# One stage between the pass that sends by src and the first spreading: a graph network on Trainium2

## The chip, the cores and the metric

The kernel runs on one core of one Trainium2 chip. The metric is the device time of one execution in microseconds (us). The engines are TensorE (PE), VectorE (DVE), ScalarE (ACT), GpSimd (POOL) and SyncE (SP), which run at the same time and meet by semaphores. SP here only issues transfers; POOL issues the indirect ones.

## The reference

There are 12,500 nodes with 48 features and 400,000 edges. Four layers follow one another, each on a layer norm of the features. Cut to what matters here, the first is:

```python
h = jnp.maximum(_layernorm(x, axis=-1), 0.0)
xw = jnp.matmul(h, w)                              # L0: project, 48 x 48
msgs = edge_weight[:, None] * xw[src]
agg = jax.ops.segment_sum(msgs, dst, num_segments=12500)
x = x + jax.nn.relu(agg + b)
# L1 also needs, for each edge, emb[node_type[src]] and emb[node_type[dst]]
# L2: two rounds of x[src] * edge_weight summed by dst; L3: three such rounds (Chebyshev)
```

## The kernel before

Nodes are held by windows of 128: node n stands in partition n % 128 of window n // 128, so a tile of all features is `[128, 98, 48]`. Edges are sorted into blocks of 8 slots for each pair of windows; 554 groups of 128 blocks hold them, 4,432 slots in each partition.
The part that the change touches stands between two long passes:

- The pass that sends by src (`recc`, `sent`, L887 to L975). SP loads records of edges two groups at a time (`recc`), ACT and DVE pick fields, and POOL sends a row of each block to `sent_dram` with 554 indirect transfers (L969).
- Stage 1 (L998 to L1052). SP loads the sent rows (`sent_in`: 554 pieces of 17 numbers in each partition). The places of dst and of src (`drel`, `srel`) are turned from partition to row: 35 tiles of each, PE transposes one 128 by 128 tile in float32 (L1023), ACT copies it to bfloat16 (L1032), SP stores it (L1042), with two buffers, so that a copy waits for the store before last. POOL gathers the type embeddings of each window (`uv`, inside `tab0`) with 98 indirect transfers (L1049).
- Stage 2 (L1601): DVE fills `X` with zeros.
- Stage 3 (`node_block`, L1088). SP loads `x` into `X`, DVE makes the layer norm (`layernorm`, L1075 to L1085) with the square root on ACT (L1104), and copies types into `rest0` and `evs`; POOL stores `evs`.
- Stage 4 (`project`, L1132). 25 spans of four windows: PE transposes (L1142), ACT copies (L1172), PE multiplies by `w0` (L1153), DVE puts the product into `rest0` (L1622).
- Stage 5: DVE splits `rest0` into three bfloat16 terms, the table `tab0` (`split`, L1194 to L1198).

Then comes the first spreading (`expand`), which multiplies one-hot matrices of places by the table, weighs the rows and sends them off, and after it the passes of the four layers.

Of the kernel before, what the change touches and what calls it, by code (L numbers as in the profile page):

```python
# [10 lines left out]
P = 128  # L11
# [64 lines left out]
def gnn_kernel(nc, x, src, dst, edge_attr, edge_weight, node_type, node_vec, w0, b0, w1, b1, w2, b2,  # L76
# [64 lines left out]
    with ctx:  # L141
# [729 lines left out]

        CS = CH * B
# [3 lines left out]
        with ExitStack() as s2:  # L876
# [12 lines left out]
            with nc.Block() as block:  # L889
                @block.sync  # L890
                def _(sp):
                    sp.dma_start(delta[:, :], delta_dram.rearrange("(a d) s -> a (d s)", a=1).to_broadcast([P, W * W])
                                 ).then_inc(s_delta, 16)

# [33 lines left out]
                def _(dve):  # L928
# [49 lines left out]
        X = sb("X", [P, W, D])  # L978
# [6 lines left out]
        s_uvg = sem("types_gathered")  # L985
        with ExitStack() as s2:
            sent_in = scoped(s2, "sent_in", [P, NG, SENT], F32)
            beyond = scoped(s2, "beyond", [P, NG], F32)

            srel_f = h1[:, :, :].rearrange("p w f -> p (w f)")[:, 0:NS]  # L990
            drel_f = X[:, :, :].rearrange("p w f -> p (w f)")[:, 0:NS]
            assert NS <= W * D
            turned = scoped(s2, "places_turned", [P, 2, P], BF16)
            ps_p = s2.enter_context(nc.psum_tensor("ps_p", [P, 2, 512], F32))
            s_ld, s_cp, s_tr, s_ev = (sem(f"rows_{n}") for n in ("load", "copied", "trans", "turned"))
            s_st = sems("rows_store", 2)
            NTR = ceil_div(NS, P)
            with nc.Block() as block:  # L998
                @block.vector
                def _(dve):  # L1000
                    dve.tensor_copy(drel_f[:, :], drel[:, :, :, 0].rearrange("p g k -> p (g k)")).then_inc(s_cp, 1)
                    dve.wait_ge(s_ld, 16)
                    dve.tensor_copy(srel_f[:, :].rearrange("p (g k) -> p g k", k=B),
                                    sent_in[:, :, 0:B]).then_inc(s_cp, 1)
                    dve.tensor_scalar(less_ident_b[:, :], ident_b[:, :], -1.0, None, ALU.mult)
                    dve.tensor_copy(slots[:, 0:NS].rearrange("p (g k) -> p g k", k=B), sent_in[:, :, B:2 * B])

                    dve.tensor_scalar(beyond[:, :], sent_in[:, :, 2 * B], 0.0, BIG, ALU.is_equal,
                                      ALU.mult).then_inc(s_cp, 1)
                    dve.wait_ge(s_cp, 3)  # L1010
                    with nc.allow_low_precision(reason="block numbers: whole, below 2^24"):
                        dve.scalar_tensor_tensor(out=idx_d[:, :], in0=sent_in[:, :, 2 * B], scalar=-1.0,
                                                 in1=beyond[:, :], op0=ALU.add, op1=ALU.add)

                @block.tensor
                def _(pe):
                    for t in range(2 * NTR):
                        of, n = (drel_f, t) if t < NTR else (srel_f, t - NTR)
                        m = min(P, NS - n * P)
                        pe.wait_ge(s_cp, 1 + t // NTR)  # L1020
                        if t >= 2:
                            pe.wait_ge(s_ev, t - 1)
                        pe.transpose(ps_p[0:m, t % 2, 0:P], of[:, n * P:n * P + m], ident[:, :]).then_inc(s_tr, 1)  # L1023

                @block.scalar
                def _(act):
                    for t in range(2 * NTR):
                        m = min(P, NS - t % NTR * P)
                        act.wait_ge(s_tr, t + 1)
# [968 lines left out]
```

## Time and profile before

| | before |
|---|---|
| median of three runs | 16256.79 us (16254.69 to 16295.25) |
| the profiled execution's own time | 16257.53 us |
| its span, first to last instruction | 16255.7 us |
| DVE busy | 12042.7 us, 74% of the span |
| PE busy | 10843.7 us, 67% |
| POOL busy | 7855.1 us, 48% |
| ACT busy | 7461.2 us, 46% |

Busy shares are means over passes of different kinds and say little about one stage; the part between the two passes is some 300 us long and is read by itself. A row of the timeline has the start, the duration, the engine, the line and the operation, and in brackets how long the engine had been idle and what released it. A row of SPq is the time that SP took to issue a transfer, and not the transfer.

### The profile page before, as it was taken

The numbers are of one execution on the slowest core, as the hardware profiler recorded it, in microseconds if no ns is written. First come the engines' busy times: TensorE is split into PE (matmuls) and PEld (weight loads), VectorE is DVE, ScalarE is ACT, GpSimd is POOL, SyncE is SP. The second block draws the span as 40 slices with busy tenths as digits, with TensorE's granted clock in tenths as the row PEclk, the third lists the DMA queues.
The fourth block names the chain that finished last, engine by engine and source line by source line (L and its number), as shares of the span: only waits on it lengthen the run. The fifth ranks groups of instructions, "written<-read, shape, count | busy, mean of one in ns | idle before, by whom it ended". The sixth has DMA issues, their size and how long they took to land. (4 is left out here: it accounts for less than half of the span.)

```text
span 16255.7 us, 582040 instructions
## 1 busy us (share of the span) xinstructions
PE 10843.7 (67%) x194032; PEld 8861.6 (55%) x194033; DVE 12042.7 (74%) x25807; ACT 7461.2 (46%) x21291; POOL 7855.1 (48%) x7665
## 2 busy tenths in 40 slices
PE   5676666666610488867776677777776686676678
PEld 4555555555500366644555556666655565565556
DVE  9666666666633378789996788789778778777776
ACT  0121212121122267744445656766664475475466
POOL 0677777777777366013331067037307605713730
PEclk8777777777755599988888888999997797798789
DMA  8343333333467499879998798889779898988987
GB/s 339 111 124 124 123 123 123 123 123 123 123 170 179 114 364 350 291 257 341 331 309 246 241 337 324 280 307 353 274 261 375 319 313 332 373 277 309 384 289 238
DMA packets 1719990, 4103.19 MB, mean 252 GB/s; under 512 B 337506, under 2 KB 626240, under 8 KB 1719094
## 3 DMA queue, kind: packets, MB, share of 16 engines
q1 hardware_dynamic: 1288470, 3065.78, 57.2%
q0 software_dynamic: 431248, 1034.11, 16.5%
q8 instruction: 80, 1.31, 0.0%
q10 hardware_dynamic: 144, 1.60, 0.0%
q14 instruction: 48, 0.39, 0.0%
HBM read 2932.16 MB, written 1702.21 MB: 285 GB/s over the span
## 5 line engine op out<-in xcount | busy, mean ns | idle before, releaser
L1443 POOL DMA_INDIRECT messages<-exp_stage,exp_block_rows x3324 | 3555.9, 1070 | 4461.9 <-ACT exp_stage L1423 1830.6
L845 POOL DMA_INDIRECT records<-rec,row_i x3125 | 3113.0, 996 | 1444.6 <-issue 814.5
L1584 PEld LDWEIGHTS sum_sums<-sum_slots,sum_onehot 128*128 128x128 bf16 x93072 | 2521.5, 96 | 1135.8 <-issue 1133.7
L1584 PE MATMUL sum_sums<-sum_slots,sum_onehot 128*128 128x48 bf16 (+1 forms) x93072 | 2677.8, 183 | 625.6 <-DVE h L1510 485.3
L1541 ACT ACTIVATE sum_onehot<-iota_b,sum_late_places 128x128 bf16<-128x128 bf16 x5817 | 1910.1, 391 | 765.1 <-PE sum_sums L1584 681.0
L1301 PE MATMUL exp_rows<-tab,h 128*128 x39888 | 1811.7, 197 | 512.7 <-DVE h L1342 225.2
L1307 PE MATMUL exp_rows<-tab,h 128*128 x13296 | 1428.4, 282 | 932.1 <-ACT exp_stage L1423 688.0
L1301 PEld LDWEIGHTS exp_rows<-tab,h 128*128 128x128 bf16 x39888 | 1567.7, 102 | 872.5 <-issue 726.5
L1307 PEld LDWEIGHTS exp_rows<-tab,h 128*128 128x128 bf16 x13296 | 1208.5, 125 | 1151.8 <-issue 1118.9
L668 ACT COPY rec<-emeta 128x40 f32 (+1 forms) x625 | 140.2, 224 | 3064.3 <-DMA records<-rec,row_i 3064.3
L1342 DVE TENSOR_SCALAR h<-exp_places,pcol 128x2048 bf16<-128x2048 bf16 x1662 | 1298.9, 782 | 164.4 <-DMA exp_places<-src_places 140.7
L789 PE MATMUL ps_l<-place_high,turned 98*128 98x98 f16 x3125 | 506.4, 258 | 1229.4 <-DVE place_low L723 1227.7
L739 DVE TENSOR_REDUCE row_i<-rank 128x5 int32<-128x490 f32 x625 | 414.0, 662 | 1206.1 <-ACT rec L668 1205.1
L1843 POOL DMA_INDIRECT messages<-l_back,l_rows x554 | 544.8, 983 | 1563.5 <-ACT l_back L1718 836.4
L1510 DVE TENSOR_TENSOR h<-h,sum_sums 128x48 f32 x3324 | 678.0, 204 | 713.4 <-PE sum_sums L1584 460.1
L1351 DVE TENSOR_TENSOR exp_times<-exp_rows,slots 128x384 f32<-128x384 f32 x1662 | 934.5, 562 | 338.7 <-PE exp_rows L1301 189.2
L1379 DVE CAST exp_stage<-exp_rows 128x576 bf16<-128x576 f32 x1380 | 990.9, 751 | 254.7 <-DMA messages<-exp_stage,exp_block_rows 181.2
L1548 ACT ACTIVATE sum_onehot<-sum_onehot,one_col 128x384 bf16<-128x384 bf16 x1939 | 1161.6, 599 | 0.0
L686 DVE TENSOR_SCALAR same<-win_row,emeta 128x640 bf16<-128x640 bf16 (+4 forms) x3125 | 1091.6, 349 | 3.3 <-DMA win_row<-src_windows_of_edges 3.3
L1402 ACT CAST exp_stage<-exp_times 128x384 bf16<-128x384 f32 x1662 | 799.2, 481 | 642.2 <-DVE exp_times L1351 623.8
L789 PEld LDWEIGHTS ps_l<-place_high,turned 98*128 98x128 f16 x3125 | 377.4, 127 | 1292.5 <-DVE place_low L723 1291.8
L1423 ACT CAST exp_stage<-exp_rows 128x576 bf16<-128x576 f32 x1662 | 992.0, 638 | 127.5 <-PE exp_rows L1307 124.0
(299 smaller groups left out, 22128.4 us busy)
## 6 DMA issues: line engine op xcount, KB each, us to landing
sum_slots<-messages SPq DMA_DIRECT2D x1662, 576.0 KB, 5.3
exp_places<-src_places SPq DMA_DIRECT2D x1662, 512.0 KB
sum_slots<-messages SPq DMA_DIRECT2D x277, 600.0 KB, 5.4
messages<-zeros SPq DMA_DIRECT2D x124, 1149.0 KB
l_places<-dst_places SPq DMA_DIRECT2D x277, 512.0 KB, 6.3
recc<-records SPq DMA_DIRECT2D x277, 448.0 KB, 4.7
l_gate<-records SPq DMA_DIRECT2D x277, 448.0 KB
records<-fill SPq DMA_DIRECT2D x215, 576.0 KB, 12.9
```

The lines of the kernel that those rows point to most:

```text
L686: return dve.tensor_scalar(same[:, g, j, j * P:K * P], win_row[:, g, j * P:K * P], emeta[:, bass.ds(n * K, K), :][:, j, SWIN:SWIN + 1], No ...
L845: pool.indirect_dma_start(rec_dram, bass.IndirectOffsetOnAxis(ap=row_i[:, g, k:k + 1], axis=0), rec[:, g, k, :], None).then_inc(put[g], 16)
L1301: last = pe.matmul(rows_at(u, a, k), of, flat[:, bass.ds(ws[c * CH + g] * (3 * width) + j * width, width)], start=j == 0, stop=j == 2)
L1307: last = pe.matmul(got[:, u % NW, k // 2, at:at + 3 * D], of, flat[:, bass.ds(ws[c * CH + g] * (3 * D), 3 * D)], start=True, stop=True)
L1342: dve.tensor_scalar(onehot[:, c % RS, :, :].rearrange("p n e -> p (n e)"), places[:, c % RP, :], pcol1[:, :], None, ALU.is_equal).then_inc ...
L1351: dve.tensor_tensor(left(u), rows_of(u, 0, D), ews[:, bass.ds(i * (2 * RG) + 2 * (c * CH + n), 2), :].unsqueeze(3) .to_broadcast([P, 2, BH ...
L1379: dve.tensor_copy(*copy_out(dve, i, first, c - 1, n)).then_inc(x_out[1], 1)
L1423: act.copy(*copy_out(act, i, first, c, n)).then_inc(x_out[0], 1)
L1443: pool.indirect_dma_start(lines, bass.IndirectOffsetOnAxis(ap=row_d[:, c, g:g + 1], axis=0), stage[:, c, g, :], None, element_offset=0 if ...
L1541: last = act.activation(late(c)[:, n, :], iota1_b[:, :], ACT.Abs, bias=late_rel[:, c, n:n + 1], scale=-1.0)
L1548: act.activation(late(c), late(c), ACT.Relu, bias=one_col[:, :], scale=-1.0).then_inc(g_late, 1)
L1584: last = pe.matmul(sums[:, c % RS, g, 0:width], onehot[:, c % RS, g * B + k, :], of[:, n * width:(n + 1) * width], start=n == 0, stop=n == ...
```

## The change

The five stages become one block of code, and the load of `x` moves into the pass ahead.

- The zeroing of `X` and the two loads of `x` go to the start of the pass that sends by src: SP issues them behind `delta` and ahead of the first `recc`.
- The places are turned in bfloat16, four tiles to one bank, one copy and one store: 10 batches instead of 35 for dst and as many for src. dst is read where it lies; src is copied to bfloat16 first.
- `project` gets `ahead` and `behind`: work of each engine before and after its own. Ahead of it stand the layer norm, the turning of dst, the load of `sent_in` and the gather of types; behind it stand the turning of src, the copies of types and the split.
- The gather is waited for by DVE behind the projection.

The core of the diff (`layernorm`, `split` and `expand` are as they were):

```diff
@@ the pass that sends by src
                     sp.dma_start(delta[:, :], ...).then_inc(s_delta, 16)
+                    sp.wait_ge(s_x0, 1)
+                    sp.dma_start(X[:, 0:W - 1, :], x[0:full].rearrange("(w p) f -> p w f", p=P)).then_inc(s_x, 16)
+                    sp.dma_start(X[0:TAIL, W - 1, :], x[full:N]).then_inc(s_x, 16)
...
+                    dve.memset(X[:, :, :], 0.0).then_inc(s_x0, 1)
                     dve.wait_ge(s_delta, 16)
@@ the stage
+                def turn_places(pe, b, of):
+                    at, many, m = batches[b % NTR]
+                    if b >= 2:
+                        pe.wait_ge(s_ev, b - 1)
+                    for j in range(many):
+                        last = pe.transpose(ps_p[0:m, b % 2, j * P:(j + 1) * P], of(at + j * P, m), ident_b[:, :])
+                    last.then_inc(s_tr, 1)
+
+                def copy_places(act, b):
+                    _, many, m = batches[b % NTR]
+                    act.wait_ge(s_tr, b + 1)
+                    if b >= 2:
+                        act.wait_ge(s_st[b % 2], 16 * (b // 2))
+                    act.copy(turned[0:m, b % 2, 0:many * P], ps_p[0:m, b % 2, 0:many * P]).then_inc(s_ev, 1)
+
+                def vector_ahead(dve):
+                    node.append(Node(dve))
+                    dve.wait_ge(s_x, 32)
+                    node[0].layernorm(h1[:, :, :], X[:, :, :], square, True)
+                    mark["x"] = node[0].c.n
+                    dve.wait_ge(s_ld, 16)
+                    dve.tensor_copy(srel_b.rearrange("p (g k) -> p g k", k=B), sent_in[:, :, 0:B]).then_inc(s_cp, 1)
...
+                def vector_behind(dve):
+                    c = node[0].c
+                    dve.wait_ge(s_uvg, 16 * W)
                     c(dve.tensor_copy(rest0[:, :, D:T0], uv[:, :, 0:G]))
                     c(dve.tensor_copy(evs[:, :, :], uv[:, :, G:2 * G]))
                     mark["evs"] = c.n
                     c.done()
+                    dve.wait_ge(s_tr, 2 * NTR)
+                    split(c, dve, tab0, rest0[:, :, :], rest0[:, :, :])
...
+                def tensor_ahead(pe):
+                    for b in range(NTR):
+                        turn_places(pe, b, lambda at, m: drel_b[:, at:at + m, 0])
+                    pe.wait_ge(v, mark["x"])
+
+                def tensor_behind(pe):
+                    pe.wait_ge(s_cp, 1)
+                    for b in range(NTR, 2 * NTR):
+                        turn_places(pe, b, lambda at, m: srel_b[:, at:at + m])
+
+                def scalar_ahead(act):
+                    for b in range(NTR):
+                        copy_places(act, b)
+                    for at, a, _ in node[0].acts:
+                        act.wait_ge(v, at)
+                        act.activation(a, a, ACT.Sqrt).then_inc(s_node, 1)
...
+                def sync_ahead(sp):
+                    sp.dma_start(sent_in,
+                                 sent_dram.rearrange("(g p) f -> p g f", p=P)).then_inc(s_ld, 16)
+                    for b in range(2 * NTR):
+                        to = drel_dram if b < NTR else srel_dram
+                        at, many, m = batches[b % NTR]
+                        sp.wait_ge(s_ev, b + 1)
+                        sp.dma_start(to[at:at + many * m, :].rearrange("(j p) e -> p j e", p=m),
+                                     turned[0:m, b % 2, 0:many * P].rearrange("p (j e) -> p j e", e=P)
+                                     ).then_inc(s_st[b % 2], 16)
```

On ACT, between the pass that sends by src and the first spreading, this stood before (`places_turned` is the buffer of turned places, `var` the variances under the root, `lhs` the turned features of a span):

```order
L1032 CAST places_turned<-ps_p 128x128 x34
L1032 CAST places_turned<-ps_p 80x128
L1032 CAST places_turned<-ps_p 128x128 x34
L1032 CAST places_turned<-ps_p 80x128
L998 UNCONDITIONAL_BRANCH
L1100 UNCONDITIONAL_BRANCH
L1104 ACT_TABLE_LOAD
L1104 ACTIVATE var<-var 128x98
L1088 UNCONDITIONAL_BRANCH
L1164 UNCONDITIONAL_BRANCH
L1172 COPY lhs<-pst 48x512 x24
L1172 COPY lhs<-pst 48x256
```

And this stands there now:

```order
L1586 COPY places_turned<-ps_p 128x512 x8
L1586 COPY places_turned<-ps_p 128x256
L1586 COPY places_turned<-ps_p 80x128
L1633 ACT_TABLE_LOAD
L1633 ACTIVATE var<-var 128x98
L1132 COPY lhs<-pst 48x512 x24
L1132 COPY lhs<-pst 48x256
L1586 COPY places_turned<-ps_p 128x512 x8
L1586 COPY places_turned<-ps_p 128x256
L1586 COPY places_turned<-ps_p 80x128
```

The root still stands behind the copies of dst, now in one block of code with them; the copies of src moved behind those of the projection.

On SP, at the start of the pass that sends by src (`delta` is a table of shifts, `recc` the records, `X` the features), this stood before and stands now:

```order
L892 DMA delta<-shift_of_blocks 128x9604
L901 DMA recc<-records 128x2x448 x6
```

```order
L895 DMA delta<-shift_of_blocks 128x9604
L898 DMA X<-in_x 128x97x48
L899 DMA X<-in_x 84x48
L907 DMA recc<-records 128x2x448 x6
```

The two loads of `X` came between the table and the first records.

## Rows read from the trace of the kernel before

**Rows 1.** Windows: stretch and length, busy us of each engine, granted clock, DMA share, GB/s.

```profile
4568.00:5298.40 730.40, 0.00 (x0) 0.00 (x0) 233.96 (x1662) 185.29 (x1385) 541.44 (x556) 0.50 0.74 186
5298.40:5596.20 297.80, 99.97 (x364) 67.92 (x364) 83.89 (x48) 34.40 (x97) 99.00 (x99) 0.50 0.37 48
5596.20:16255.70 10659.50, 7685.44 (x164872) 6232.83 (x164872) 8487.08 (x15640) 6415.00 (x17281) 4100.63 (x3878) 0.87 0.88 311
```

**Rows 2.** Timeline around the start of stage 1: start, duration, engine, line, operation.

```profile
5298.58 0.85 SPq L1036 DMA_DIRECT2D sent_in<-laces_weights_and_blocks  x1
...
5301.88 52.29 SPq L1042 DMA_DIRECT2D dst_places<-places_turned  x1
...
5355.88 2.77 POOL L1049 DMA_INDIRECT tab<-table_types,types_i  x1 [0.30 <-issue]
5356.07 2.47 DVE L1003 COPY h<-sent_in 128x4432 f32<-128x4432 f32 x1 [55.05 <-DMA sent_in<-laces_weights_and_blocks]
5357.19 0.64 ACT L1032 CAST places_turned<-ps_p 128x128 bf16<-128x128 f32 x2 [55.12 <-DMA dst_places<-places_turned]
```

**Rows 3.** The tile `places_turned`: its copies on ACT, durations in ns, first and last start.

```profile
L1032 ACT CAST places_turned<-ps_p x70: 262/266/267, 5301.6 to 5422.8; 128x128 bf16<-128x128 f32 x68, 80x128 bf16<-80x128 f32 x2
```

**Rows 4.** The end of stage 1 (L998) on POOL's queue: duration in ns, start.

```profile
L998 POOLq DRAIN  x1: 8045/8045/8045, 5429.1 to 5429.1; - x1
```

**Rows 5.** Timeline of stages 2 and 3, zeroing, load and layer norm.

```profile
5438.40 3.98 DVE L1604 MEMSET X<- 128x4704 f32 x1 [75.66 <-issue]
5442.66 1.28 ACT L1104 ACT_TABLE_LOAD   x1 [19.63 <-PEq L1601]
5442.72 11.66 SPq L1109 DMA_DIRECT2D X<-in_x  x2
5456.28 5.05 DVE L1075 TENSOR_REDUCE mean<-X 128x98 f32<-128x4704 f32 x1 [13.90 <-DMA X<-in_x]
...
5477.13 0.29 ACT L1104 ACTIVATE var<-var 128x98 f32<-128x98 f32 x1 [33.19 <-DVE var L1080]
...
5483.42 2.61 DVE L1085 TENSOR_SCALAR h<-h 128x4704 f32<-128x4704 f32 x1
...
5487.77 1.79 DVE L1614 COPY evs<-tab 128x3136 f32<-128x3136 f32 x1
```

**Rows 6.** Timeline of stage 4, the projection, its first and last work.

```profile
5495.93 1.87 PE L1142 MATMUL pst<-ident,h 128*48 128x128 f32 x8 [74.30 <-PEq L1088]
5496.98 0.58 ACT L1172 COPY lhs<-pst 48x512 f32<-48x512 f32 x1 [19.57 <-PE pst L1142]
...
5565.61 0.26 DVE L1622 COPY rest<-pso 128x96 f32<-128x96 f32 x1 [0.50 <-PE pso L1153]
```

**Rows 7.** Timeline of stage 5, the split, and the first load behind it.

```profile
5566.19 4.25 DVE L1194 CAST tab<-rest 128x7840 bf16<-128x7840 f32 x1 [0.32 <-PEq L1132]
...
5591.46 4.24 DVE L1198 CAST tab<-rest 128x7840 bf16<-128x7840 f32 x1
5596.19 13.69 SPq L1254 DMA_DIRECT2D exp_places<-src_places  x7
```

**Rows 8.** Windows: DVE's five operations on the sent rows, and the projection.

```profile
5356.00:5366.00 10.00, 4.10 (x10) 1.82 (x10) 6.64 (x5) 2.66 (x10) 8.78 (x5) 0.50 0.22 46
5496.00:5566.00 70.00, 69.57 (x294) 55.22 (x294) 8.84 (x25) 14.26 (x25) 0.00 (x0) 0.50 0.00 1
```

**Rows 9.** Timeline of the pass that sends by src, its first and last work.

```profile
4583.58 0.22 ACT L913 COPY sent<-recc 128x16 f32<-128x16 f32 x1 [53.89 <-DMA recc<-records]
...
4585.34 1.01 POOL L969 DMA_INDIRECT laces_weights_and_blocks<-sent,row_s  x1 [16.06 <-ACT drel L917]
...
5293.14 0.97 POOL L969 DMA_INDIRECT laces_weights_and_blocks<-sent,row_s  x1 [0.30 <-issue]
```

**Rows 10.** That pass's indirect transfers on POOL, durations in ns, first and last start.

```profile
L969 POOL DMA_INDIRECT laces_weights_and_blocks<-sent,row_s x554: 971/972/1070, 4585.3 to 5293.1; - x185
```

**Rows 11.** Transfers issued at 4566 to 4584 us: number, size, us to landing.

```profile
delta<-shift_of_blocks SPq DMA_DIRECT2D x1, 4802.0 KB, 14.2
```

More of the change, by code:

```diff
@@ L870, in windows @@
                 skip_runtime_bounds_check_because="windows are counted below W")[1]
+        X = sb("X", [P, W, D])
+        s_x0, s_x = sem("x_zeroed"), sem("x_load")
+        full = (W - 1) * P
         CS = CH * B
@@ L1121, in gnn_kernel, with project @@
         n_pj = [0]
-        def project(parts, put, room=None):
+        def project(parts, put, room=None, ahead={}, behind={}):
             base = PT * n_pj[0]
@@ L1132, in project, with _ @@
                 with nc.Block() as block:
+                    @block.vector
+                    def _(dve):
+                        if "vector" in ahead:
+                            ahead["vector"](dve)
+                        for n, (w0, w1) in enumerate(spans):
+                            dve.wait_ge(pj_prod, base + n + 1)
+                            put(dve, pso[:, n % 2, 0:(w1 - w0) * D].rearrange("p (w f) -> p w f", f=D),
+                                slice(w0, w1)).then_inc(pj_out, 1)
+                        if "vector" in behind:
+                            dve.wait_ge(pj_out, base + PT)
+                            behind["vector"](dve)
+                    if "sync" in ahead:
+                        block.sync(ahead["sync"])
+                    if "gpsimd" in ahead:
+                        block.gpsimd(ahead["gpsimd"])
                     @block.tensor
@@ L1173, in _ @@
                             last.then_inc(pj_lhs, 1)
-                    @block.vector
-                    def _(dve):
-                        for n, (w0, w1) in enumerate(spans):
-                            dve.wait_ge(pj_prod, base + n + 1)
-                            put(dve, pso[:, n % 2, 0:(w1 - w0) * D].rearrange("p (w f) -> p w f", f=D),
-                                slice(w0, w1)).then_inc(pj_out, 1)
+                        if "scalar" in behind:
+                            behind["scalar"](act)
         x_ld, x_st = sems("exp_load", RC), sems("exp_store", RC)
@@ L1589, in _ @@
                         turns_and_rest(pe, TURNS, REST, turn)
-        full = (W - 1) * P
+        s_uvg, s_evs = sem("types_gathered"), sem("dst_embedding_stored")
+        s_ld, s_cp, s_tr, s_ev = (sem(f"rows_{n}") for n in ("load", "copied", "trans", "turned"))
+        s_st = sems("rows_store", 2)
         with first:
@@ new lines, in gnn_kernel @@
+                batches = [(t * P, min(4, tiles - t), P) for t in range(0, tiles, 4)]
+                if NS % P:
+                    batches.append((tiles * P, 1, NS % P))
+                NTR = len(batches)
+                def turn_places(pe, b, of):
[5 more added lines that the diff above has]
+                    last.then_inc(s_tr, 1)
```

130 lines of the change are left out of this document (48 added, 82 removed).

## The prediction

> **What bounds the kernel now.** I read the windows first, to see how much time the change can reach [rows 1]. The part between the pass that sends by src and the first spreading is 297.8 us long, and in it no engine is busy for more than 100 us (DVE 83.9, PE 100.0, POOL 99.0). It is a chain of waits, not one busy engine, so putting its pieces beside each other can pay. The 10,659.5 us behind it are not touched: the instructions are the same, and so are the addresses of their tiles. The sum is therefore about 300 us plus the pass ahead, into which the load of `x` goes.
>
> Then I followed the part in order of time. SP issues the load of the sent rows at 5298.6, and the first store of turned places, issued behind it, holds SP for 52.29 us. Data arrive at 5356.07 on DVE, and ACT gets its first store back at 5357.19 after 55.12 us of idleness [rows 2]. So for 57 us everything that needs a store or the sent rows stands still. The other 68 copies then take until 5422.8, 65.6 us for 34 pairs, 1.93 us a pair [rows 3]: a round trip of a store. POOL's gather ends at 5429.1, when its end-of-block drain of 8.05 us begins [rows 4]. Zeroing, load and layer norm follow from 5438.4, with DVE beginning on data at 5456.28 and ending the copies of types at 5489.6 [rows 5]. The projection runs from 5495.93 to 5565.87 [rows 6], the split to 5595.70, and the first spreading starts at 5596.19 [rows 7].
>
> **The change, step by step.** All times are those of the trace before; a shift of the pass ahead is added at the end.
>
> *Layer norm.* `x` is there, so DVE starts at about 5298.6. Its first part, up to the root, lasts 5477.13 − 5456.28 = 20.85 us [rows 5] and ends at 5319.5. The root is ACT's, and there it stands behind ten copies of dst places. The third of them waits for the first store, which is still issued behind the load of the sent rows. So the root can't run before 5357.2 [rows 2]: half of what the layer norm could gain is lost, and this new wait decides the stage.
>
> *Turning of dst.* Ten batches. A copy of 512 columns takes 0.58 us [rows 6] in place of 0.27. A store has 512 pieces in place of 128; the load of `x`, with 12,416 pieces, held SP for 11.66 us [rows 5], 0.94 ns a piece, so 384 more pieces are 0.36 us, and two stores are under way. A pair takes 1.93 + 0.31 + 2 × 0.36 = 2.96; I take 2.9 us. No row shows such a store: from below a pair costs 2.2 (only the copy grows), from above 4 × 1.93 = 7.7. It is nearest to the sum, since pieces of the same kind are priced. The copies are then at 5357.8 (two), 5360.7, 5363.6 and 5366.5, the last ends at 5367.3.
>
> *Root and rest.* The table load of 1.28 us stands behind the copies now, where it was hidden before by the load of `x`: root at 5368.6. From root to the end of the layer norm it takes 5486.03 − 5477.13 = 8.9 us [rows 5]: 5377.5.
>
> *Projection.* PE starts at 5377.7 and the last put ends 69.94 us later [rows 6], at 5447.6. DVE first has 6.64 us of work on the sent rows [rows 8], which have arrived, until about 5384.4; the first product comes 3.8 us after PE's start and the third would need its put at 5387, so this is hidden. Without that cover it would cost up to 6.6 us.
>
> *Gather.* POOL's 98 transfers run beside it and are landed by 5429.1, 18 us before DVE asks. DVE's copies from and to memory hold POOL up: beside one of 2.47 us a transfer took 2.77 us in place of 0.94 [rows 2]. If every DVE operation of the layer norm and on the sent rows shut POOL out (some 36 us, of which some 6 are in the trace already), the gather would be 30 us later, at 5459, and the copies of types with it, at 5462.5: 4 us on the end. [...] I take nothing, and 4 as a bound.
>
> *Turning of src.* It stands behind the projection. Types are copied in 3.5 us, to 5451.1. PE is free at about 5447.2, ACT copies the first pair at 5447.9, the next pairs at 5450.8, 5453.7 and 5456.6, and PE's last transposes end at about 5458.2. The split waits for them, since it writes over `srel_b`: 7 us of new wait. It then takes 29.5 us [rows 7]: 5487.7, and 0.5 to the first load of the spreading, 5488.2. POOL's store of `evs` and its drain (14 us from 5451) and SP's last stores lie under the split.
>
> Gain of the part: 5596.2 − 5488.2 = 108.0 us.
>
> *The load of `x` in the pass ahead.* That pass is POOL's: 554 transfers of 0.97 us, with 0.30 between them, are 705 us, and from first to last it takes 708.8 [rows 9, 10]. What delays its first transfer is not caught up. It begins when the first records land at 4583.6, just behind `delta`, which takes 14.2 us to land [rows 11]. Now 2.4 MB of `x` in small pieces stand between the two on the same queue. Zeroing (4 us) is hidden by `delta`; of the 13.9 us that `x` took from issue to landing, the transfer's 11.7 come on top, plus a second start-up of about 1.3, as the records' issue is held until `x` is nearly through. I take 13 us. From below 0 (all under `delta`), from above 17.9 (zeroing and load as they stood, 5438.4 to 5456.3).
>
> Sum: −108.0 + 13 = −95 us. The profiled execution took 16257.5 us, 0.7 above the median of the three runs: 16162.5, as a median 16162.
>
> **The rivals.**
>
> 1. *The root isn't held* (the change does more): if the stores got past the load of the sent rows, the layer norm would end at 5328.4 and PE would do two spans and wait for DVE, which is busy with the sent rows until 5362.7. The projection would end at about 5427.5, the types at 5432.6, src at 5438.7, the split at 5468.2: 19.5 us less, 16143. Against it: the same order on SP gave ACT 55.12 us of idleness [rows 2]. 4%.
>
> 2. *The projection runs at full clock.* The granted clock was 0.50, 1.2 GHz, throughout, though PE was busy for 69.57 of 70 us [rows 8]. At 2.4 GHz it would last some 35 us; the gather (5429.1) would then end last, the types at 5432.6, and the split at 5462: 26 us less, 16137. For it: the work on either side of the projection is new. Against it: nothing keeps PE busier than before; ahead of it are ten small batches and 10 us of idleness. 5%. The Trainium skill, "TensorE: Matmul & The Clock Gate", part 1, has a TensorE that is kept busy go to full clock. By that rule it would have done so in the 70 us here; the row disagrees.
>
> 3. *The stores of four rows a partition cost as four* (7.7 us a pair): dst ends 14.4 us later, and src as much: 16191. 5%.
>
> 4. *Slower than before*: such a store is cut into its single numbers, 65,536 pieces, 62 us each at 0.94 ns. The twenty stores, one behind the other on SP's queue, cost 1.2 ms: about 17,390. It decides once a store costs 4.8 us more than I take (95 / 20), and the loss can be measured from 7.2. Against it: a store's last dimension is a whole row of 128 as before, and one such store of 128 rows went through in half of 1.93 us [rows 3]. 1%.
>
> **How the numbers follow.** The forecast with its bounds has 83%: 16162, with 13 us less if `x` costs nothing, 5 more if it costs all, 5 less for pairs of 2.2 us, 4 more for POOL, and 10 each way for waits that I have not seen; its own range is 16143 to 16185. Rivals 1 and 2 lie below, 3 above; the range of 16138 to 16190 holds the first and the third and leaves about 12% out. The runs before spread by 0.25%; less than 0.3% (49 us) can't be told from no change. Faster by more than that needs a time below 16208, which all but rival 4, a far larger price of stores or of `x`, and passes behind that run differently for no reason seen here would give: 94% faster, 4% same, 2% slower.
>
> **What would show it.** In the trace after: DVE idle from some 21 us after the start of the stage until its reciprocal, some 70 us after it, released by ACT's root; ACT's third copy released by the first store at about 59 us; PE's first `pst` at 79 us; the split at about 160 us, released by PE's transposes of src; the stage about 190 us long in place of 298. In the pass ahead, ACT's first copy about 28 us after its start in place of 15.6. The prediction is wrong if the root runs before the sent rows land, if pairs of stores take over 5 us, if the pass ahead grows by over 20 us, or if the first spreading is not as long as before.

## The result, and the profile after

| | forecast | measured |
|---|---|---|
| median | 16162 | 16215.16 us (18 executions; 16213.76 without the one named below); before, beside them, 16267.15 (18) |
| ratio to before, 95% interval | 0.994 | 0.9955 [0.9945, 0.9966] |
| profiled execution, its span | 16162 | 16156.63 us, 16154.8 us |
| the stage | 190 us | 190.4 us |
| passes behind it | as before | 10652.2 us |

The change makes the kernel faster, by 0.45%, but the median lies 53 us above the forecast and outside the range, while the profiled execution lies 5 us below it. One execution of 28151 us is left out of what follows, and so are three more far above the rest in the experiments, of 18608 us in e7, 18393 in e8 and 18905 in r16.

The windows of the kernel after, cut as in [rows 1]:

```profile
4569.70:5312.20 742.50, 0.03 (x1) 0.06 (x2) 237.83 (x1664) 184.98 (x1385) 541.88 (x556) 0.50 0.75 186
5312.20:5502.60 190.40, 79.90 (x364) 61.48 (x364) 77.47 (x46) 26.02 (x47) 111.40 (x99) 0.50 0.51 63
5502.60:16154.80 10652.20, 7682.34 (x164872) 6246.90 (x164872) 8451.71 (x15640) 6417.58 (x17281) 4116.27 (x3878) 0.87 0.88 311
```

The stage went from 297.8 us to 190.4, and the pass ahead from 730.4 to 742.5, 0.2 us of it by where the cuts lie. The rest is 7.3 us shorter, on the same work, and nothing here says why. With 1.7 us more ahead of the first cut that makes the 100.9 us between the two profiled executions: −107.4 + 12.1 − 7.3 + 1.7.

Timeline of the pass ahead and of the stage:

```profile
4569.73 0.33 SPq L895 DMA_DIRECT2D delta<-shift_of_blocks  x1
4574.85 0.85 SPq L898 DMA_DIRECT2D X<-in_x  x1
4575.75 17.35 SPq L899 DMA_DIRECT2D X<-in_x  x1
...
4596.63 0.22 ACT L919 COPY sent<-recc 128x16 f32<-128x16 f32 x1 [65.30 <-DMA recc<-records]
...
4598.40 1.01 POOL L976 DMA_INDIRECT laces_weights_and_blocks<-sent,row_s  x1 [27.41 <-DVE row_s L950]
...
5312.17 5.05 DVE L1012 TENSOR_REDUCE mean<-X 128x98 f32<-128x4704 f32 x1 [17.55 <-PEq L892]
5312.19 0.77 SPq L1640 DMA_DIRECT2D sent_in<-laces_weights_and_blocks  x1
5312.79 1.07 ACT L1586 COPY places_turned<-ps_p 128x512 bf16<-128x512 bf16 x2 [18.51 <-PE ps_p L1578]
...
5313.40 53.78 SPq L1646 DMA_DIRECT2D dst_places<-places_turned  x1
...
5316.65 0.94 POOL L1654 DMA_INDIRECT tab<-table_types,types_i  x1 [0.30 <-issue]
...
5317.66 5.06 DVE L1014 TENSOR_TENSOR h<-X,mean 128x4704 f32<-128x4704 f32 x1
5317.90 5.64 POOL L1654 DMA_INDIRECT tab<-table_types,types_i  x1 [0.30 <-issue]
...
5370.24 1.07 ACT L1586 COPY places_turned<-ps_p 128x512 bf16<-128x512 bf16 x2 [56.38 <-DMA dst_places<-places_turned]
...
5380.38 1.28 ACT L1633 ACT_TABLE_LOAD   x1
...
5381.68 0.28 ACT L1633 ACTIVATE var<-var 128x98 f32<-128x98 f32 x1
5382.07 0.77 DVE L1019 RECIPROCAL var<-var 128x98 f32<-128x98 f32 x1 [48.92 <-ACT var L1633]
...
5390.63 1.90 PE L1096 MATMUL pst<-ident,h 128*48 128x128 f32 x8 [12.13 <-DVE h L1022]
...
5452.26 0.94 POOL L1654 DMA_INDIRECT tab<-table_types,types_i  x1 [0.30 <-issue]
...
5460.34 0.26 DVE L1663 COPY sent_in<-pso 128x96 f32<-128x96 f32 x1 [0.49 <-PE pso L1107]
5460.63 1.79 DVE L1610 COPY sent_in<-tab 128x3136 f32<-128x3136 f32 x1
...
5472.61 4.24 DVE L1150 CAST tab<-sent_in 128x7840 bf16<-128x7840 f32 x1 [8.48 <-PE ps_p L1578]
...
5502.61 1.32 SPq L1210 DMA_DIRECT2D exp_places<-src_places  x3
```

In the pass ahead SP waits 5.1 us for the zeroing and is then held by `X` for 17.35 us. ACT starts 26.9 us behind `delta`'s issue in place of 15.6, POOL 28.7 in place of 17.3 [rows 1, 9]: both 11.3 us later (13 forecast), and the pass is 11.9 us longer. In the stage it is the chain that the prediction describes. The first store holds SP, ACT's third copy waits for it, the root stands behind the ten copies and a table load, and DVE is idle for 48.92 us. The split then waits 8.48 us for PE's turning of src.

So the stage holds what was foreseen. The missing 53 us are in the times of the single executions. (About 10 of them are already in the kernel before, whose median was 16256.79 when the forecast was made and 16267.15 here.) Those of the kernel after lie in two groups, 6 from 16150 to 16177 us and 11 from 16207 to 16236, medians 16160.7 and 16230.0. Those of the kernel before do too: 13 from 16243 to 16279 and 5 from 16290 to 16316, medians 16257.7 and 16306.2. In the lower groups the difference is 97.0 us. Before's are parted less clearly, by a gap of 10 us where that of after is 30. But the median of before is one of its lower group, and that of after one of its upper.

The place was found by laying an execution of the upper group (the profiled one of e1, below) beside one of the lower. The windows of PE in the last projection, just ahead of the output, are first those of the kernel after (16156.63 us, lower group), with stretch, length, busy us and granted clock:

```profile
16057.60:16073.20 15.60, 1.37 (x48) 0.68 0.00 1
16073.20:16139.20 66.00, 65.96 (x588) 0.97 0.00 1
```

and those of the same kernel in e1 (18810.42 us, upper group):

```profile
18653.30:18668.90 15.60, 1.37 (x49) 0.65 0.00 1
18668.90:18791.30 122.40, 122.40 (x588) 0.50 0.00 1
```

PE does 588 multiplications without a pause in both. In one they take 66 us at a granted clock of 0.97, in the other 122 at 0.50 (1.0 is 2.4 GHz, 0.50 is 1.2 GHz). Both begin at 0.50; the first stands at 1.00 from 16077 us on, 4 us into its work, and the second never rises. That is 56 us, and in the sets of runs shown here the groups' medians lie 49 to 71 us apart, most of them 53 to 62. Ahead of it PE is idle for 14.2 us, while DVE works on the nodes. The other traces without added work of PE ahead of this projection agree: in e2 and r13, both executions of an upper group, it took 122 us at 0.50, and in those of before, e3, e4 and e12, all of a lower group, 66 us.

### The profile page after: what moved, and what is told of

The parts are those of the page before. It is cut to its first block and busy times, and to the rows that moved or that the text cites. A ratio compares the mean times of both kernels' runs of the same rounds, so it can differ in the third digit from the quotient of the medians.

```text
span 16154.8 us, 581780 instructions
## 1 busy us (share of the span) xinstructions
PE 10820.7 (67%) x194032; PEld 8866.5 (55%) x194033; DVE 12006.3 (74%) x25806; ACT 7455.3 (46%) x21241; POOL 7887.2 (49%) x7665
```

## The experiments

Each set of kernels ran on one chip, beside the kernel before. Two kinds of chip came up. On the first the kernel before takes 16.27 ms and the new stage 190 us; on the second 18.6 to 18.8 ms and 235 us. e5 to e8, r17 and r18 ran on chips of the first kind, all others on the second. e1 to e4 were designed when the two groups had been seen, but not their place. A lower group is compared with a lower one, and an upper with an upper.

**e1_again**: the kernel after, unchanged.

> The changed kernel unchanged, for more runs and a second trace. Its trace on record shows the stage 190 us long in place of 298 and a time of 16157 us, yet 11 of its 17 undisturbed runs lie between 16206 and 16236 and 6 between 16150 and 16177. Theory A: the stage gains some 100 us in every run, and an event of some 65 us elsewhere in the program comes in some runs, in two groups again and nothing between 16180 and 16200; if this trace is one of the upper group, the 65 us stand outside the stage, with a lower granted clock there. Theory B: the stage itself has two speeds; then a trace of the upper group shows the stage some 250 us long.

18808.92 us, 0.9983 [0.9971, 0.9995]; 4 runs in a lower group (median 18759.1) and 8 in an upper one (18815.6), against 25 (18820.6) and 10 (18875.7) of the kernel before. Within the groups the change gives 60 us. Theory A holds: the difference lies outside the stage, with a clock of 0.50, and is 56 us, not 65. Its stage took 235.0 us in place of 190.4, for another reason (the pauses below), and its pass ahead 877.0.

**e2_root_first**: the copies of dst behind the root on ACT.

```diff
                 def scalar_ahead(act):
-                    for b in range(NTR):
-                        copy_places(act, b)
                     for at, a, _ in node[0].acts:
                         act.wait_ge(v, at)
                         act.activation(a, a, ACT.Sqrt).then_inc(s_node, 1)
+                    for b in range(NTR):
+                        copy_places(act, b)
```

> The root of the first layer norm stands ahead of ACT's ten copies of dst places. By the reading that the root is held by the stores behind the load of the sent rows: DVE's reciprocal comes 21 us after the stage's start in place of 70, but PE's transposes of dst still end 66 us after it, so the projection starts 12 us earlier and the stage takes 178 us: 12 us less than the changed kernel. Rival: the root isn't what holds the projection, no change within 3 us. By theory A the runs fall in two groups 65 us apart again, each 12 us lower.

18771.21 us, 0.9973 [0.9960, 0.9986]. Its lower group (8 runs, 18767.0) is 8 us above e1's, the upper one (4, 18825.2) 10 above: nothing gained here, where 12 us were expected. The projection started 67 us after the stage's start, as expected, but took 136 us, and the stage 245.5.

**e3_x_in_stage**: zeroing and load of `x` at the start of the stage, ahead of the sent rows.

> Zeroing and load of x stand at the start of the stage again, ahead of the load of the sent rows on SP; the rest as changed. The pass ahead is 13 us shorter (POOL's first transfer 17 us after its start), the stage 16 us longer (206 us): 3 us slower than the changed kernel, group by group. If x in the pass ahead is what makes the upper group frequent (theory C), the upper group is as rare as in the kernel before (5 of 18); if not, it stays above half.

18752.19 us, 0.9965 [0.9952, 0.9979]; groups of 7 (18743.5) and 5 (18802.3), 16 and 13 us below e1's, where 3 above were expected. Its pass ahead took 865.7 us, 11.3 less than e1's, which is the term of `x`. But its stage, expected 16 us longer, took 229.4 in place of 235.0.

**e4_x_only**: the kernel before with zeroing and load of `x` in the pass ahead and nothing else.

> The kernel before with the load of x alone moved into the pass ahead (dst places are copied for turning into a free part of tab0). The pass ahead grows by 13 us; zeroing, its block's end (5 us) and the wait for the load (14 us), 18 us in all from the end of stage 1 to the layer norm, go: 5 us faster than before in each group. By theory C the upper group is frequent here, by theories A and B as rare as in the kernel before.

18831.71 us, 1.0002 [0.9989, 1.0016]: no difference, where 5 us less were expected. Its pass ahead took 874.5 us and the five stages 305.9. The gain is that of the new stage, not of the moved load. Its upper group holds 3 of 12 runs and that of e3 5 of 12, so `x` in the pass ahead doesn't make the upper group frequent (theory C).

**e5_warm_before to e8_warm_root** test whether the last projection's clock makes the groups. PE is kept at work ahead of it, by 56 multiplications whose results nobody reads (the filler):

```diff
+                        for _ in range(filler):
+                            pe.matmul(kept[:, :], ident_b[:, :], flat[:, 0:512], start=True, stop=True)
...
-        node_block(steps)
+        node_block(steps, filler=56)
```

> The kernel before with one addition: in the last block on the nodes, ahead of the last projection, PE works through 56 multiplications of 512 bfloat16 columns whose results nobody reads; before, it was idle there for 14.2 us. Theory: every kernel here has two groups of times some 57 us apart because the last projection runs either at a granted clock of 1.0 (62 us) or of 0.50 (119 us), and with PE at work ahead of it it starts at 1.0 each time. Then all runs lie within 20 us of each other, at the kernel before's lower group or up to 8 us below it, and no run is 57 us above; the profile shows the last projection in 55 to 62 us at clock 1.0. Rival: the two groups come from another pass and the clock of the last projection only goes along with it; then two groups some 57 us apart remain, and the projection lasts about 60 us in both.

> The kernel after with the same 56 multiplications ahead of the last projection. Theory: one group again, 8 us or less below the kernel after's lower group. Against the run of the kernel before with the same addition, the change is then seen without the two groups: 95 to 99 us less, as in the profiled executions (16257.5 to 16156.6 is 101), on a chip like that of the first runs; 60 us less on one like that of the second, where the stage was 235 us long in place of 190. Rival: the change costs something in passes behind it that the profiled execution didn't show; then the difference to the kernel before with the addition is 50 us or less where the stage is 190 us long.

> The kernel after with both: 56 such multiplications ahead of the last projection and 48 ahead of the new stage's projection, behind the turning of dst, where PE waits some 10 us for the layer norm. Theory A: the clock at a projection's start decides what it keeps. The stage's projection then runs at 1.0 in 40 us in place of 70, POOL's gather (landed 141 us after the stage's start) ends last, the split starts at 145 us in place of 160, and the kernel is 15 us faster than with the last one alone. Theory B: the projection by itself doesn't hold 1.0, as it never rose in 70 us of work: the clock falls back to 0.50 within some microseconds, and the stage is at most 5 us shorter; the time stays within 5 us of that with the last one alone.

> The kernel after with the 56 multiplications ahead of the last projection, and ACT's root ahead of its copies of dst places. Theory: the root no longer stands behind the first store, so PE's projection starts right behind the turning of dst, 68 us after the stage's start in place of 78.5: 10 us less than with the multiplications alone, as POOL's gather (141 us) then ends 3 us behind the projection's end (138) and bounds it, 7 to 10 us in all. Rival: the layer norm's second half, now beside the first wait, holds POOL's gather up by as much again, and nothing or less than 4 us is gained.

| | runs | median | lowest, highest |
|---|---|---|---|
| before | 12 and 5 | 16266.5 and 16320.9 | 16243.1, 16335.9 |
| e5, before + filler | 12 | 16265.5 | 16258.8, 16284.4 |
| e6, after + filler | 6 | 16169.7 | 16161.9, 16177.4 |
| e7, also ahead of the first projection | 5 | 16159.0 | 16157.2, 16167.6 |
| e8, e6 + root first | 5 | 16159.8 | 16135.1, 16173.6 |

The upper group is gone in all four, and in all later runs with the filler: none of the 71 executions that remain without the three named above stands 50 us above the lowest of its set, and in all twelve traces with the filler the last projection took 64 to 65 us. e6's windows, PE's filler and the last projection:

```profile
16081.50:16094.70 13.20, 12.14 (x54) 1.00 0.00 0
16094.70:16159.50 64.80, 64.12 (x588) 1.00 0.01 1
```

e5 and e6 differ by 95.8 us: free of the groups, the change is worth what was forecast (95). The up to 8 us below the lower group didn't come: the projection took 64.8 us in place of 66.0. e5's runs lie 26 us apart, not 20, and e7 and e6, whose stages are alike, differ by 10.7 us, so the 95.8 may be off by as much.

In e7 the first projection starts at 1.0, after a filler of its own, and doesn't keep it (windows of all engines, the granted clock third from the end; then PE's timeline):

```profile
5376.00:5389.00 13.00, 12.77 (x60) 6.12 (x58) 10.79 (x4) 2.89 (x5) 11.78 (x5) 0.88 0.07 14
5389.00:5403.00 14.00, 11.67 (x59) 9.33 (x59) 5.98 (x10) 2.88 (x5) 11.22 (x10) 0.63 0.11 21
5403.00:5457.00 54.00, 53.91 (x232) 43.07 (x232) 7.79 (x21) 10.69 (x21) 34.92 (x37) 0.50 0.11 24
```

```profile
5374.78 12.40 PE L1632 MATMUL kept_ahead<-slots,ident_b 128*128 128x512 bf16 x47 [0.22 <-issue]
5387.01 1.04 PE L1105 MATMUL pst<-ident,h 128*48 128x128 f32 x8
...
5390.87 0.62 PE L1105 MATMUL pst<-ident,h 128*48 128x128 f32 x4
5393.82 1.91 PE L1116 MATMUL pso<-w_sb,lhs 48*128 48x48 f32 x8 [2.33 <-issue]
```

Its stage took 192.6 us, e6's 191.2: nothing gained, as theory B expects. But the clock didn't fall in unbroken work. PE did 4.5 us of the projection at 1.00 and then waited 2.33 us. DVE was still working on the sent rows and put its first product away only at 5393.36. Behind that wait the clock was 0.50 (0.91 from 5391 to 5393, 0.50 from 5393 to 5395), and it didn't rise again, with PE busy for 53.91 of 54 us. So e7 shows that this work doesn't leave 0.50. Whether it would keep 1.0 without the wait wasn't tested. The 10.7 us between the medians lie outside the stage and are not explained by this edit.

In e8 the root runs at 21 us, and DVE waits for POOL's gather instead:

```profile
5336.69 0.28 ACT L1640 ACTIVATE var<-var 128x98 f32<-128x98 f32 x1 [19.75 <-DVE var L1017]
...
5458.89 1.79 DVE L1619 COPY sent_in<-tab 128x3136 f32<-128x3136 f32 x1 [6.42 <-DMA tab<-table_types,types_i]
5460.60 1.78 DVE L1620 COPY sent_in<-tab 128x3136 f32<-128x3136 f32 x1
5462.42 4.24 DVE L1159 CAST tab<-sent_in 128x7840 bf16<-128x7840 f32 x1
```

Stage 176.7 us, 14.5 less than e6; medians 9.9 less. The stage gained more than the 7 to 10 us expected, and PE's turning of src no longer holds the split. The whole time tells less: e7, whose stage gained nothing, stands as low. Against the kernel before the ratios are 0.9924 [0.9905, 0.9944] for e8, 0.9927 [0.9908, 0.9946] for e7 and 0.9931 [0.9914, 0.9948] for e6. e8 has the shortest stage of all, and no measured time shows it to be better than e6.

**e9 to e12** went on with the load of `x`, the best order, and PE's idleness. e11 issues `x` behind the first turn's records:

```diff
                             sp.dma_start(recc[:, c, :, :].rearrange("p (g k) f -> p g (k f)", k=B),
                                          slot_rows[:, bass.ds(i * RG + c * CH, CH), :]).then_inc(ld[c], 16)
+                        if first:
+                            sp.wait_ge(s_x0, 1)
+                            sp.dma_start(X[:, 0:W - 1, :], x[0:full].rearrange("(w p) f -> p w f", p=P)).then_inc(s_x, 16)
+                            sp.dma_start(X[0:TAIL, W - 1, :], x[full:N]).then_inc(s_x, 16)
```

> The kernel after with the 56 multiplications ahead of the last projection, but with the zeroing of X and the load of x at the start of the new stage, ahead of the load of the sent rows. Theory of the prediction (x costs 13 us in the pass ahead, where nothing catches it up; 11.3 in the profiled execution): ACT's first copy comes 15.6 us after the pass's start in place of 26.9, the pass is 11 us shorter, and in the stage the sent rows and the first store land some 14 us later, 71 us after its start in place of 59: the two cancel to within 3 us. Rival: POOL's pass has slack for a late start; then the pass ahead is as long as with x in it, and the kernel is 11 to 14 us slower than with the multiplications alone.

> The kernel before with the 56 multiplications and only one part of the change: zeroing and load of x in the pass that sends by src. The five stages stay apart. Theory: the pass ahead grows by 11 to 13 us, and zeroing and load of 17.9 us leave the part between the two passes, so 5 to 7 us less than the kernel before with the multiplications: within 0.1%. Rival: x hides under the pass ahead in most executions and the 17.9 us are all gained; or it costs more than in the profiled one, and the kernel is slower.

> The kernel after with the 56 multiplications, the root ahead of ACT's copies, and the load of x issued behind the first twelve groups of records instead of ahead of them. Theory: the first records come at once, the pass ahead is up to 11 us shorter, less some 2 to 6 us where the records behind x come late (SP needs 17.4 us to issue x, and six pairs of groups last about 15.6 us), so 5 to 9 us less than with the root ahead alone. Rival: it only moves the wait; POOL stands still for some 11 us in the first turn but one, and nothing is gained.

> The kernel after without the multiplications, in which DVE copies t2 five times in place of once in the block ahead of the last projection: 4 times 2.7, so 10.8 us more in which PE is idle, 25 us in place of 14.2. Theory A: the longer PE was idle before it, the surer the last projection stays at 0.50; all or nearly all runs are then in an upper group, 57 us + 11 us above the lower one of the kernel after. Theory B: the length of the idle time doesn't matter and the start of the projection falls by chance to one or the other side; then a share of the runs between a third and two thirds is in the upper group, as in the kernel after.

Medians, beside the kernel before in groups of 20 (18822.8) and 5 (18884.3): e9 18754.7 (6 runs), e10 18825.8 (12), e11 18764.1 (8), e12 groups of 8 (18776.5) and 4 (18842.0). From `delta`'s issue to the stage's first transfer e9 took 865.6 us, e11 866.6, e12 872.5 and e10 875.4: without `x` ahead of the records the pass is 6 to 10 us shorter, less than the term of 11 to 13. The 14 us that e9's stage should lose for it didn't show in its length: 230.6 us from the issue of `x`, against 235.1 in e12. The projection did start 12 us later in e9 (110.1 us after the stage's start, against 97.8), but took 78 us in place of 95. e10 stands 3 us above the lower group of the kernel before and not 5 to 7 below: no gain, as in e4. e9 and e11 have no run of the kernel after with the filler beside them, which r14 and r15 supply. e12 decides for its theory B: 10.8 us more of idleness ahead of the last projection made the upper group no larger, 4 of 12 (PE idle for 24.93 us in its trace, and the projection at 66 us even so).

**r13 to r16** asked the same once more, with the kernel after beside them. The 878 us that r14's rival names for e9 run to the load of the sent rows; to the stage's first transfer it is 865.6.

> The kernel after as it is. Theory A: the change raises the share of runs whose last projection stays at 0.50; about half or more of them are then some 57 us above the rest, against a quarter of those of the kernel before (25 of the 95 runs so far). Theory B: the share is a matter of the single launch and the same for both, about a quarter to a third; the 11 of 17 in the runs of the result were chance.

> The kernel after with the 56 multiplications and the load of x in the stage, once more, beside r16 on the same chip. Prediction's term: the pass ahead is 11 to 13 us shorter than with x in it and the stage 11 to 14 us longer, within 3 us in all where the stage has no pauses. Rival (as on the chips with pauses, where the pass was 878 us with and without x): the pass is no shorter, and the kernel is 11 to 14 us slower than r16.

> Root first, the 56 multiplications, and x behind the first twelve groups of records. Where POOL is the pass ahead's only limit: 5 to 9 us less than the 14.5 us that the root first alone took from the stage, so some 20 us below r16. Rival: POOL stands still some 11 us while x is loaded; then 14 us below r16 at most. Where the projection is paused beside POOL's gather: no gain over r16, as the projection then begins earlier and more of the gather runs beside it.

> The kernel after with the 56 multiplications, as the measure for r14 and r15 on the same chip. One group of times; 95 us below the lower group of the kernel before where the stage is 190 us long, and about 60 where it is 235.

| | runs | median | pass ahead | stage |
|---|---|---|---|---|
| before | 9 and 8 | 18579.5 and 18632.2 | | |
| r13, after | 6 and 6 | 18500.0 and 18570.6 | 863.8 | 234.6 |
| r14, `x` in the stage | 6 | 18486.9 | 859.0 | 229.4 |
| r15, root first, `x` later | 6 | 18502.2 | 860.2 | 245.2 |
| r16, after + filler | 5 | 18497.8 | 871.0 | 234.5 |

r13 and r16 have the same pass ahead and differ by 7 us in it, so a term of 11 us can't be read here from single traces. r14 stands 11 us below r16, where no more than 3 either way were expected. r15 stands 4 us above it: no gain, which is its third case, the paused projection. r16 stands 82 us below the lower group of before, not 60. In r13 the upper group holds 6 of 12 runs and in before beside it 8 of 17, so theory A finds no support there. What these chips show is another thing. Windows of PE in the first projection, of e10 (five stages, no gather beside it), then of r16, r14 and e11:

```profile
6610.00:6679.00 69.00, 69.00 (x294) 0.50 0.00 1
```

```profile
6373.40:6468.00 94.60, 69.73 (x295) 0.50 0.06 12
```

```profile
6374.00:6452.00 78.00, 69.87 (x298) 0.50 0.04 9
```

```profile
6463.00:6599.00 136.00, 69.80 (x299) 0.50 0.08 17
```

The work is 69 to 70 us each time, and the rest is idleness: none, 25, 8 and 66 us. It lies beside the gather or just behind it. POOL's last transfer of the gather starts at 6416.2 in r16, 6399.2 in r14 and 6536.6 in e11, and from some 11 us later PE is busy for 41.00 of 41 us, 42.00 of 42 and 51.37 of 52. In one such pause of e11 POOL's transfers go on and all others stand still:

```profile
6487.00:6517.00 30.00, 2.89 (x12) 2.26 (x12) 0.36 (x1) 0.58 (x1) 22.68 (x25) 0.50 0.13 26
```

The more of POOL's gather runs beside the projection, the longer it takes: 25 us of it beside 8 us of idleness in r14, 43 beside 25 in r16, 74 beside 66 in e11. With the root first, more does, and the stage takes 245 us in place of 235 (e2 beside e1, r15 beside r16). The copies of dst pause as well: in e1 they take 29.6 us from the first store's return, against 10.1 in the trace of the kernel after, so of the 45 us that the stage is longer there, 19 are lost before the projection begins.

**r17_gather_before and r18_root_first_look** kept the gather out of the projection (PE waits for `s_uvg` as well as for the layer norm).

> The kernel with the 56 multiplications and the root first, in which PE starts the projection only when all of POOL's gather has landed. Theory: the pauses of PE, ACT and DVE come with POOL's transfers; PE is then idle for less than 2 us inside the projection, which lasts 68 us on any chip, and the stage is about 141 + 68 + 46 = 255 us long. Rival: the pauses are those of a chip whatever POOL does; PE is idle for 25 to 66 us inside the projection here too, if the run beside it shows them.

> The 56 multiplications and the root first, as the measure for r17: on a chip with pauses a projection of some 133 us with 66 us in which PE is idle, and a stage of 245 us; on one without, 68 us, none, and 177 us.

They met a chip without pauses. r17's stage took 255.1 us (255 expected), r18's 176.8, the executions 16227.32 and 16155.86 us, each of one execution, and PE was idle for less than 1 us in either projection. In r18 the gather ran beside the whole projection, as in e11 beside 74 us of it, and made no pause, so the gather alone doesn't make them. The 78 us between the two stages are the price of the wait. Whether the wait removes the pauses where there are some wasn't seen.

## Why the prediction was right in its steps and wrong in its number

- **What bounds the part**: right, a chain of waits. All times from the stage's start, forecast and measured: first store back 59 and 58.1; copies from there to the last 10.1 and 10.1; reciprocal 70 and 69.9; PE's first `pst` 79 and 78.5; split 160 and 160.4, behind PE's turning of src; end 190 and 190.4. 108.0 us were to be gained; 107.4 were.
- **Stores of four rows a partition**: right. A pair took 2.6 to 3.1 us for dst (2.9 forecast), and for src 2.6, 2.6 and 5.0, the last while POOL stored `evs`; the split waited 8.48 us for it, 7 forecast. Rivals 3 and 4 fall.
- **Rival 1** (the root isn't held) falls by the 48.92 us of idleness. e8 frees the root in another way, and the copies still wait for the first store, so PE's projection began 66 us after the start. It gained 14.5 us in the stage. The 19.5 us worked out for stores that get past the load were not tested.
- **Rival 2** (projection at full clock): the clock was 0.50 throughout. e7 gave it 1.0 at the start, and it fell at a wait of 2.33 us. By "TensorE: Matmul & The Clock Gate", part 1, of the Trainium skill a TensorE that is kept busy goes to full clock. The last projection did so in some executions and not in others; this one stayed at 0.50 while PE was busy for 53.91 of 54 us, so the rule as I put it fails here.
- **POOL's gather**: "I take nothing, and 4 as a bound" was right for the end, but no row of before shows that the gather would hardly move, and it did: its last transfer ended on POOL 141 us after the start in place of 130.5. A transfer took 5.64 us beside a `TENSOR_TENSOR` of 5.06 in the stage's timeline, and 0.94 otherwise. The Trainium skill, "SBUF — State Buffer", section "Who interferes with whom", has a DVE instruction with two inputs in SBUF contend with a GpSimd instruction that reads SBUF, but also says that a probe showed no DMA stalled by `tensor_tensor`. The trace decides against the second: both inputs were in SBUF, and POOL's transfer was held up. It cost nothing because the projection ended 7 us later still. In e8, where the projection ends earlier, it cost 6.42 us.
- **`x` in the pass ahead**: 13 us forecast; the first transfer came 11.3 us later and the pass was 11.9 longer, so the term was 1 to 2 us too large. The other traces on chips of the first kind agree: 730.9 us without `x` in the pass (e5), 741.0 to 742.6 with it (e6, e7, e8, r17, r18).
- **Two slips** that change nothing: the 65.6 us hold some 33 pairs of copies and not 34, so a pair took 1.96 us; and the range up to 16190 leaves out the third rival, 16191, by 1 us.
- **The step that failed** is "The profiled execution took 16257.5 us, 0.7 above the median of the three runs: 16162.5, as a median 16162". It took one execution's distance to a median of three for a property of the kernel, and so took the passes behind the stage at nothing for the median too. The kernel has two values some 56 us apart, by the clock of its last projection. Of the three runs of before two were of the lower one, and the median with them. Of the kernel after, 11 of 17 executions were of the upper, and its median with them. So the medians set a lower execution against an upper one, and differ by 52 us and not by 95. e5 and e6 show the cause: with PE kept at work ahead of that projection no execution is of an upper group, and the change measures 95.8 us. That these passes "are not touched" was true of their instructions. The prediction gave "passes behind that run differently for no reason seen here" a part of its last 6%, and its range had no case for a clock that differs from one execution to the next. That the profiled execution came within 5 us of the forecast is in part luck: it happened to be of the lower group, as before's was, and 7.3 us came from passes that the sum doesn't hold.

**What stays open.** Why the last projection's clock rises in one execution and not in the next. Whether the change itself raises the share of the upper group: for the kernel after it was 11 of 17, 8 of 12 and 6 of 12, for the one before beside it 5 of 18, 10 of 35 and 8 of 17. By those three sets together, 25 of 41 against 23 of 70, chance alone is a poor explanation, but the close variants e2, e3 and e12 had 4, 5 and 4 of 12. The length of PE's idleness ahead of it isn't the reason (e12). What the pauses on the second kind of chip are, and whether the gather causes them, wasn't settled either; they take away part of the gain there, 60 to 80 us in the lower groups in place of 97. The traces show only that those of the projection lie beside POOL's gather or just behind it.

## What to carry to other kernels

Before a difference of some 50 us is forecast, look at every stretch in which PE alone sets the pace behind an idle one: read its granted clock, and ask what the kernel would take at the other level. A sum of terms from one profiled execution forecasts that execution; the median needs the runs' distribution, and three runs don't show it. When a wait is broken up, order the engine's list by who is waited for: the root ahead of the copies gave 14.5 us in the trace for two lines moved. Then run it on more than one chip: on the other kind the same lines made the stage 10 us longer.

## What was not expected of the hardware

- The same 588 multiplications, without a pause, took 66 us (clock 0.97) or 122 us (0.50) in the same kernel. Work of 56 unread multiplications over PE's 14 us of idleness ahead of them removed the slower case in all 71 executions that are counted here with it. It cost no time that can be seen: e5's median is that of the kernel before's lower group.
- Unbroken work doesn't always bring the clock up: the first projection, with 48 rows, stayed at 0.50 with PE busy for 69.57 of 70 us [rows 8], and after one wait of 2.33 us for 53.91 of 54 us (e7). The last one, with 96 rows, stayed at 1.00 for 64.80 us when it began there (e6).
- `TENSOR_TENSOR` on two operands in SBUF held up POOL's issue of an indirect transfer for its whole length: 5.64 us beside 5.06. Beside a `TENSOR_REDUCE` of 5.05 us the transfers kept 0.94 to 1.00 us.
- Chips differ in more than pace: on the second kind PE, ACT and DVE paused together for up to 30 us while POOL issued transfers, and an edit that took 14.5 us from the stage on the first kind (root first) added 10 to it there, and 8 to 10 us to the times of each group (e2 beside e1).
